# Three of four normalised row pairs of each attention batch, turned by VectorE blocks and device memory instead of by TensorE

## The chip, the cores and the metric

The kernel runs on one core of a Trainium2 chip. The metric is the device time of one execution in microseconds (us). The core has a matrix engine (TensorE, PE), a vector engine (VectorE, DVE), a scalar engine (ScalarE, ACT), GpSimd (POOL), and SyncE (SP), which here issues every transfer. Each engine works through its own program in order, and they wait for each other by semaphores.

## The reference

One hybrid layer over 2 batches of 1024 tokens with 512 columns, kept in float32:

```python
x = x + attn_a(_layernorm(x))     # gated linear attention, in chunks of 128 tokens
x = x + ffn(_layernorm(x))        # first feed-forward
x = x + attn_b(_layernorm(x))     # softmax attention, 1 head of 512 columns
x = x + ffn(_layernorm(x))        # second feed-forward, the same weights
```

where `attn_b` is

```python
scores = jnp.einsum('bqe,bke->bqk', Q, K) * scale
attn = jax.nn.softmax(scores, axis=-1)
out = jnp.einsum('bqk,bke->bqe', attn, V)
return jnp.einsum('bse,ed->bsd', out, W_o)
```

and `ffn` is `qlinear(silu(gate) * up)` with a hidden width of 1408.

## The kernel before

The program runs through stages: A (linear attention, both batches), F1 (feed-forward, batch 0 and 1), B (softmax attention, batch 0 and 1), F2 (feed-forward, batch 0 and 1). A float32 operand is split into a high and a low float16 part, and each product is three matmuls (high by high, high by low, low by high). The scores and the first feed-forward products use a recursive scheme of seven block products ("pieces" 1 to 7) in which sums and differences of the column blocks of an operand stand in for it.

Every stage takes its rows normalised and turned (features on partitions). One batch is 8 row tiles of 128 tokens, taken as 4 pairs (`i` = 0 to 3, two rows per pair). Six sets of pairs exist: F0, F1, B0, B1, F2, F3. For a pair, DVE takes row statistics (`x_stats`, three instructions), POOL the inverse deviation (`x_rstd`), DVE normalises both rows into the tile `xn` (`x_normalise`), the pair is turned, ACT takes its high parts (`x_row_highs`, `x_12_high`, `x_34_high`), DVE and POOL form differences and low parts (`x_second`, `x_34_low` on DVE; `x_sums`, `x_ab_low`, `x_12_low` on POOL).

There are two ways to turn. In the sets of `MOVED` (F1, B0, F3, prepared beside a feed-forward stage), DVE transposes 32x32 blocks in place, and SP sends the blocks to device memory and fetches them back in turned order, four DMAs out and four back (a "set" of four each way). In F0, B1 and F2, TensorE turns the pair: `turn_x` is four 128x128 transposes into one PSUM bank for each of the two rows (`turn_both(i)` is both), and ACT first copies the first row out of PSUM (`x_copy`).

B1 is prepared while batch 0 is in stage B, and F2 while batch 1 is. In stage B every engine's order is written out by hand, the same for both batches. For each of 8 query tiles there is a tile of probabilities: TensorE forms the scores (`first_row(p)` is pieces 1, 2, 6, 5, 3 for the tiles 2p and 2p + 1, then `score(7, p)` and `score(4, p)`), ACT and DVE add the pieces in `probs[i % 2]` (`part_sum`, `part_add`), DVE takes the row maximum, ACT the exponential (`softmax(i)`), DVE the block transpose (`p_blocks(i)`), SP sends it out and back, ACT and DVE split it (`pT_high`, `pT_low`), and TensorE multiplies it with the values (`attend(i)`). Piece 1, 6, 7 and 4 share PSUM bank 4, which is free again when the `part_sum` of the piece before has run. SP's queue holds the transfers of the probability tiles in strict order: out, wait, back.

## Time and profile before

| | before |
|---|---|
| median of 3 runs | 935.93 us (935.61 to 936.5) |
| the profiled execution's own time | 935.47 us |
| its span, first to last instruction | 933.7 us |
| PE busy | 919.0 us (98%) |
| DVE busy | 632.7 us (68%) |
| ACT busy | 444.5 us (48%) |
| POOL busy | 432.9 us (46%) |
| stage B, batch 0 and batch 1 | about 479 to 599 us and 604 to 719 us of the span |

The span leaves out some 1.8 us around the first and the last instruction. "Busy" is the time in which an engine had an instruction in work; a wait inside a stage shows as a gap in the timeline, with the instruction that ended it.

### The profile page before, as it was taken

What the parts mean: (1) busy time and instruction counts of PE and PEld (TensorE: products, weight loads), DVE (VectorE), ACT (ScalarE), POOL (GpSimd) and SP (SyncE); (2) the same over time, 40 slices, a digit from 0 to 9 for tenths busy, and PEclk for the clock granted to TensorE, in tenths of its full rate; (3) what the DMA queues carried; (4) which work ended last, traced back from release to release, by engine and by line L of the source; (5) the groups of instructions that cost most, each with busy time, mean ns of one, the idle gap of its engine ahead of it and who ended that gap; (6) DMA issues with size and microseconds to landing.
All of it is one profiled execution on the core that took longest, in us unless ns stands there. A gap on an engine that the chain in (4) does not pass through costs nothing.

```text
span 933.7 us, 13067 instructions
## 1 busy us (share of the span) xinstructions
PE 919.0 (98%) x4550; PEld 512.7 (55%) x4550; DVE 632.7 (68%) x1171; ACT 444.5 (48%) x884; POOL 432.9 (46%) x448
## 2 busy tenths in 40 slices
PE   7999999999999999999999999999999999999998
PEld 4888988888743444444444444444444444444444
DVE  7555656948777687777755878547786777765643
ACT  4433334356577723764333345324454685346620
POOL 5433524377446654665640144420535566546530
PEclk9999999999999999999999999999999999999999
DMA  9401300024031181003713637216371001910001
GB/s 319 179 12 35 136 24 24 1 90 138 25 111 46 24 131 28 1 11 63 109 46 56 104 53 147 48 26 97 59 113 24 1 1 32 194 45 1 1 34 57
DMA packets 239952, 61.75 MB, mean 66 GB/s; under 512 B 226768, under 2 KB 227088, under 8 KB 239504
## 3 DMA queue, kind: packets, MB, share of 16 engines
q1 hardware_dynamic: 239888, 60.92, 29.1%
q8 instruction: 37, 0.61, 0.3%
q14 instruction: 27, 0.22, 0.1%
HBM read 41.47 MB, written 19.43 MB: 65 GB/s over the span
## 4 chain that ended last, share of the span: by engine, by line
PE 85%; DVE 7%; POOL 2%; ACT 2%; issue 2%; DMA 1%; SPq 0%; DVEq 0%; ACTq 0%; POOLq 0%
PE psum L2327 49%; PE psum L2574 14%; PE psum L2576 14%; PE psum L2724 6%; DVE ln_bn L1620 1%; PE psum L2376 1%; DVE even_lo L2211 1%; PE psum L2461 1%; PE psum L2365 1%; DVE probs L2207 1%; DVE s_f L2155 0%; ACT probs L1493 0%; DVE wv_lo L1711 0%; DMA xres<-x 0%; DVE smax L2200 0%
## 5 line engine op out<-in xcount | busy, mean ns | idle before, releaser
L1038 POOL TENSOR_TENSOR hid<-hid,hid_hi 128x512 f32<-128x512 f32 x88 | 102.8, 1169 | 103.9 <-DVE hid_hi L1976 103.9
L2574 PE MATMUL psum<-xf,w_gu 128*128 128x512 f16 x352 | 133.8, 380 | 0.5 <-DVE yt L2058 0.5
L2574 PE MATMUL psum<-xf,w_s 128*128 128x512 f16 x264 | 100.1, 379 | 1.5 <-DVE up L1949 1.3
L2576 PE MATMUL psum<-xf,w_gu 128*128 128x512 f16 x264 | 100.1, 379 | 0.0
L2327 PE MATMUL psum<-wd_low,hid_lo 128*128 128x512 bf16 (+1 forms) x330 | 73.8, 373 | 0.0
L1361 ACT ACTIVATE hid_lo<-hid 128x512 f16<-128x512 f32 x88 | 54.9, 624 | 33.2 <-POOL hid L1038 33.2
L1034 POOL TENSOR_TENSOR hid<-up,gate 128x512 f32<-128x512 f32 x44 | 56.0, 1273 | 25.3 <-ACT gate L1356 25.3
L2576 PE MATMUL psum<-xq,w_s 128*128 128x512 f16 x176 | 66.7, 379 | 0.0
L2574 PEld LDWEIGHTS psum<-xf,w_gu 128*128 128x128 f16 x352 | 34.3, 98 | 55.0 <-ACT acc L1346 15.5
L1356 ACT ACTIVATE gate<-gate,sg_xs 128x512 f32<-128x512 f32 x44 | 31.7, 721 | 58.5 <-DVE gate L1959 58.5
L2327 PEld LDWEIGHTS psum<-wd_low,hid_lo 128*128 128x128 f16 x330 | 32.3, 98 | 36.8
L1941 DVE TENSOR_TENSOR gate<-psum,acc 128x512 f32<-128x512 f32 x44 | 30.4, 692 | 31.2 <-ACT acc L1334 23.5
L1976 DVE TENSOR_SCALAR hid_hi<-hid 128x512 f16<-128x512 f32 x88 | 39.1, 444 | 16.0 <-POOL hid L1034 14.5
L900 POOL TENSOR_TENSOR xrstd<-xvar,minus_half 128x1 f32<-128x1 f32 x48 | 25.2, 550 | 52.5 <-DVE xvar L1624 52.4
L2327 PE MATMUL psum<-wd_b,hid_hi 128*128 128x512 bf16 (+1 forms) x198 | 48.1, 373 | 0.0
L2574 PEld LDWEIGHTS psum<-xf,w_s 128*128 128x128 f16 x264 | 25.9, 98 | 35.7 <-issue 4.7
L1959 DVE TENSOR_TENSOR gate<-psum,acc 128x512 f32<-128x512 f32 x44 | 30.4, 691 | 20.4 <-PE psum L2576 20.1
L2576 PEld LDWEIGHTS psum<-xf,w_gu 128*128 128x128 f16 x264 | 25.8, 98 | 30.8
L1968 DVE SCALAR_TENSOR_TENSOR hid<-psum,su_c,gate 128x512 f32<-128x512 f32 x44 | 33.0, 750 | 12.5 <-PE psum L2576 12.5
L2327 PE MATMUL psum<-wd_a,hid_hi 128*128 128x512 bf16 (+1 forms) x165 | 39.9, 373 | 0.0
L2058 DVE TENSOR_TENSOR yt<-psum,sd_rows 128x512 f32<-128x512 f32 x31 | 21.1, 688 | 27.6 <-PE psum L2327 27.2
L1949 DVE SCALAR_TENSOR_TENSOR up<-psum,su_c,acc 128x512 f32<-128x512 f32 x44 | 33.0, 749 | 9.1 <-POOL hid L1034 7.6
(354 smaller groups left out, 2417.5 us busy)
## 6 DMA issues: line engine op xcount, KB each, us to landing
prob_blocks<-probs SPq DMA_DIRECT2D x60, 128.0 KB, 2.7
back<-prob_blocks SPq DMA_DIRECT2D x40, 128.0 KB, 2.8
turned<-blocks SPq DMA_DIRECT2D x36, 128.0 KB, 3.0
cla_wide<-cla_dram SPq DMA_DIRECT2D x16, 256.0 KB, 3.2
out<-xres SPq DMA_DIRECT2D x15, 256.0 KB, 2.0
xres<-x SPq DMA_DIRECT2D x3, 1024.0 KB, 12.9
blocks<-xn SPq DMA_DIRECT2D x24, 128.0 KB, 3.0
codes_gu<-gateT SPq DMA_DIRECT2D x1, 2816.0 KB, 11.7
```

Source lines behind the costliest of these rows:

```text
L1034: nc.gpsimd.tensor_tensor(hid2[:, :], up2[:, :], gate2[:, :], ALU.mult).then_inc(hid2_done, 1)
L1038: nc.gpsimd.tensor_tensor(hid[:, :], hid[:, :], hid_part(hid_hi, j, half), ALU.subtract).then_inc(rest_done, 1)
L1356: nc.scalar.activation(gate2[:, :], gate2[:, :], ACT.Silu, scale=sg_xs[:, j:j + 1]).then_inc(silu2_done, 1)
L1361: nc.scalar.activation(hid_part(hid_lo, j, half), hid[:, :], ACT.Copy, scale=LO).then_inc(lo_done, 1)
L1941: nc.vector.tensor_tensor(cols(gate1, j % 2), bank(2), acc1[:, :], ALU.add).then_inc(drained[2], 1)
L1949: nc.vector.scalar_tensor_tensor(out=up2[:, :], in0=bank(3 + j % 2), scalar=su_c[:, j:j + 1], in1=acc3[:, :], op0=ALU.mult, op1=ALU.add).t ...
L1968: nc.vector.scalar_tensor_tensor(out=hid1[:, :], in0=bank(j % 2), scalar=su_c[:, j:j + 1], in1=cols(gate1, j % 2), op0=ALU.mult, op1=ALU.m ...
L1976: nc.vector.tensor_scalar(hid_part(hid_hi, j, half), hid[:, :], ROUND, -ROUND, ALU.add, ALU.add).then_inc(hi_done, 1)
L2327: return nc.tensor.matmul(out, lhsT, rhs, start=start, stop=stop)
L2574: nc.tensor.matmul(bank(use[0]), w, x_operand(piece, k, False), start=start and k == 0, stop=False, skip_group_check=not start)
L2576: last = nc.tensor.matmul(bank(use[0]), w, x_operand(piece, k, True), start=False, stop=k == 1, skip_group_check=not start)
L2724: last = nc.tensor.matmul(bank(use[0]), l, r, start=start and k == 0 and j == 0, stop=k == 1 and j == 2, skip_group_check=not start)
```

## The change

For the pairs 0, 1 and 2 of B1 and F2 (`SENT = 3`) the transposes of TensorE go. DVE transposes the blocks of `xn` in place (`pair_turned`), SP sends them to a new buffer in device memory (`pair_to_dram`) and fetches them into the tile `x_first` of the set, which is made two rows wide (`pair_to_slot`); both rows are then read from there and no longer from PSUM. There is one such tile per set, so pair 1 is fetched only when all readers of pair 0 are done. Pair 3 is turned by TensorE as before. The normalised tile `xn` is still the only one, so each pair's `x_normalise` waits until the pair before has gone out. The second half of the new tile of B1's set covers `sd_rows`, which is therefore loaded a second time (`down_scales`). The orders of SP, DVE, ACT, POOL and PE in stage B are rewritten around it.

```diff
+SENT = 3
+            def pair_to_slot(q, i):
+
+                n = 4 * q + i
+                sp.wait_ge(pair_out, sent_all(q, i))
+                if i > 0:
+                    sp.wait_ge(x_ab_lo, n)
+                    sp.wait_ge(x_t34_done, 2 * n)
+                    sp.wait_ge(pair_2_lo, sent_n(q, i))
...
             query_parts(0, 0)
-            x_rstd(B1, *range(4))
+            x_rstd(B1, *range(6))
             query_parts(0, 1)
-            x_rstd(B1, *range(4, 8))
+            x_rstd(B1, *range(6, 8))
             pairs_of(B1)
...
+            def pair_turned(q, i):
+                dve.wait_ge(ln_xn_done, ln_n("X", q, 2 * i + 1) + 1)
+                nc.vector.transpose(xn[:, :], xn[:, :]).then_inc(pair_blocks_done, 1)
+
             def x_normalise(q, i):
+                if q in (B1, F2) and i > 0:
+                    dve.wait_ge(pair_out, sent_all(q, i - 1))
...
                 attend(1)
-                turn_both(0)
                 first_row(2)
                 attend(2, 0, 4)
                 score(7, 2)
                 attend(2, 4, 8)
                 score(4, 2)
-                turn_both(1)
                 first_row(3)
                 attend(3)
-                turn_both(2)
                 attend(4, 0, 4)
```

On PE the three `turn_both` go from each batch and nothing else moves. Three other places follow, all in batch 0; batch 1 has the same rows with its own tiles.

The queue of SP from the sending of probability tile 2 on, before (`probs_205` and `probs_206` are the two tiles `probs`, `back_207` and `back_208` those they come back to; x4 is one set of four DMAs):

```order
L854 DMA prob_blocks<-probs_205 32x32x32 x4
L865 DMA back_207<-prob_blocks 128x8x32 x4
L854 DMA prob_blocks<-probs_206 32x32x32 x4
L865 DMA back_208<-prob_blocks 128x8x32 x4
L854 DMA prob_blocks<-probs_205 32x32x32 x4
L865 DMA back_207<-prob_blocks 128x8x32 x4
```

and now (`x_first_141` is the two rows wide tile of set B1):

```order
L873 DMA prob_blocks<-probs_205 32x32x32 x4
L896 DMA pair_blocks<-xn 32x32x32 x4
L888 DMA back_207<-prob_blocks 128x8x32 x4
L873 DMA prob_blocks<-probs_206 32x32x32 x4
L896 DMA pair_blocks<-xn 32x32x32 x4
L912 DMA x_first_141<-pair_blocks 128x8x32 x4
L888 DMA back_208<-prob_blocks 128x8x32 x4
L896 DMA pair_blocks<-xn 32x32x32 x4
L912 DMA x_first_141<-pair_blocks 128x8x32 x4
L873 DMA prob_blocks<-probs_205 32x32x32 x4
L888 DMA back_207<-prob_blocks 128x8x32 x4
```

Between tile 2 and tile 4 the queue gets three sets out and two sets back for the pairs, and the fetch of pair 1 stands ahead of the sending of tile 4.

The order of ACT from the exponential of tile 4 to the score piece 1 of the tiles 6 and 7, before (L1488 is `part_sum`, L1493 `softmax`):

```order
L1493 ACTIVATE probs_205,rowsum<-probs_205,nmax,mids 128x1024
L1488 ACTIVATE probs_206<-psum 128x512 x2
L1488 ACTIVATE probs_205<-psum 128x512
L1493 ACTIVATE probs_206,rowsum<-probs_206,nmax,mids 128x1024
L1488 ACTIVATE probs_205<-psum 128x512
L1156 ACTIVATE x_first_141<-psum 128x512
```

and now (L1566 is `part_sum`, L1571 `softmax`, L1245 and L1247 are the high parts of pair 1):

```order
L1571 ACTIVATE probs_205,rowsum<-probs_205,nmax,mids 128x1024
L1566 ACTIVATE probs_206<-psum 128x512
L1245 ACTIVATE xb_hi_57<-x_first_141 128x4x128
L1247 ACTIVATE xb_hi_57<-x_first_141 128x4x128
L1566 ACTIVATE probs_206<-psum 128x512
L1566 ACTIVATE probs_205<-psum 128x512
L1258 ACTIVATE xs_hi_61<-x_mid_145 128x4x128
```

The two copies of pair 1 now stand between the two `part_sum` of `probs_206`, that of piece 7 and that of piece 4.

The order of DVE from the first `part_add` of the tiles 4 and 5 on, before (L1665 to L1670 are `x_second(0)`, L2188 and L2190 `part_add`):

```order
L2190 TENSOR_TENSOR probs_205<-psum,probs_205 128x512
L1665 TENSOR_TENSOR x_mid_145<-psum,x_first_141 128x256
L1668 TENSOR_TENSOR x_mid_145<-psum,x_mid_145 128x256
L1670 TENSOR_TENSOR xb_lo_59<-psum,xb_hi_57 128x4x128
L2188 TENSOR_TENSOR probs_205<-psum,probs_205 128x512
L2190 TENSOR_TENSOR probs_205<-psum,probs_205 128x512
L2200 TENSOR_REDUCE smax<-probs_205 128x1
L2202 TENSOR_SCALAR nmax<-smax,mids 128x1
L1630 TENSOR_SCALAR xn<-xres,xmv,xrstd 128x512 x2
```

and now (L1752 to L1757 are `x_second(0)`):

```order
L2277 TENSOR_TENSOR probs_205<-psum,probs_205 128x512
L1752 TENSOR_TENSOR x_mid_145<-x_first_141 128x256
L1755 TENSOR_TENSOR x_mid_145<-x_first_141,x_mid_145 128x256
L1757 TENSOR_TENSOR xb_lo_59<-x_first_141,xb_hi_57 128x4x128
L1698 BN_STATS ln_bn<-xres 128x6
L1700 BN_AGGR xmv<-ln_bn 128x2
L1702 TENSOR_SCALAR xvar<-xmv 128x1
L1698 BN_STATS ln_bn<-xres 128x6
L1700 BN_AGGR xmv<-ln_bn 128x2
L1702 TENSOR_SCALAR xvar<-xmv 128x1
L2275 TENSOR_TENSOR probs_205<-psum,probs_205 128x512
L2277 TENSOR_TENSOR probs_205<-psum,probs_205 128x512
```

The statistics of the last two rows, which stood with those of the rows 4 and 5 ahead of the query parts, now come behind `x_second(0)`. On POOL the inverse deviations of these rows stand ahead of `x_sums(0)` in both kernels.

## Rows read from the trace of the kernel before

**Rows 1.** The page, part 1: busy time, share of the span, instructions.

```profile
PE 919.0 (98%) x4550; PEld 512.7 (55%) x4550; DVE 632.7 (68%) x1171; ACT 444.5 (48%) x884; POOL 432.9 (46%) x448
```

**Rows 2.** Waits of PE: us in total, times, longest.

```profile
PE psum L2327 <- DVE even_lo L2211: 2.3, 3, 0.8
```

**Rows 3.** Groups by line and shape, PE: busy us, mean ns, idle before.

```profile
L2376 PE MATMUL psum<-ident,xn 128*128 128x128 f32 x96 | 13.5, 274 | 0.5 <-DVE a_lo L2159 0.5
```

**Rows 4.** Timeline of PE: start us, us, count, idle before.

```profile
4.05 4.45 PE L2327 MATMUL psum<-mask_b,ident_b 128*128 128x512 bf16 x10 [4.05 <-POOL mask_b L941]
...
515.31 0.38 PE L2724 MATMUL psum<-xb_hi,s_lo 128*128 128x512 f16 x1
516.51 0.38 PE L2327 MATMUL psum<-v_hi,even_hi 128*128 128x512 f16 x1 [0.82 <-DVE even_lo L2211]
...
539.81 0.60 PE L2376 MATMUL psum<-ident,xn 128*128 128x128 f32 x4
...
541.11 0.38 PE L2724 MATMUL psum<-xb_hi,a_hi 128*128 128x512 f16 x1
...
555.36 1.04 PE L2376 MATMUL psum<-ident,xn 128*128 128x128 f32 x8
556.30 0.38 PE L2724 MATMUL psum<-xb_hi,a_hi 128*128 128x512 f16 x1
```

**Rows 5.** Timeline of DVE, batch 0 of stage B.

```profile
530.08 0.65 DVE L1620 BATCH_NORM_STATS2 ln_bn<-xres 128x6 f32<-128x512 f32 x1
...
534.10 0.42 DVE L2152 SCALAR_TENSOR_TENSOR s_f<-psum,a_f 128x256 f32<-128x256 f32 x1
...
537.57 1.87 DVE L2155 TENSOR_TENSOR s_f<-s_f,a_f 128x256 f32<-128x256 f32 x1
...
539.82 0.68 DVE L2159 SCALAR_TENSOR_TENSOR a_lo<-psum,a_hi 128x512 f16<-128x512 f32 x1
...
550.70 1.00 DVE L1630 TENSOR_SCALAR xn<-xres,xmv,xrstd 128x512 f32<-128x512 f32 x2
552.18 1.25 DVE L2207 STREAM_TRANSPOSE probs<-probs 128x1024 f32<-128x1024 f32 x1 [0.49 <-ACT probs L1493]
...
555.05 0.21 DVE L2221 TENSOR_SCALAR mids<-rowsum,mids 128x1 f32<-128x1 f32 x1
...
556.16 0.68 DVE L2190 TENSOR_TENSOR probs<-psum,probs 128x512 f32<-128x512 f32 x1
```

**Rows 6.** Timeline of POOL, batch 0 of stage B.

```profile
536.62 2.55 POOL L1102 TENSOR_TENSOR s_lo<-s_f,s_hi 128x1024 f16<-128x1024 f32 x1 [2.72 <-ACT s_hi L1472]
...
541.07 2.13 POOL L1102 TENSOR_TENSOR s_lo<-s_f,s_hi 128x1024 f16<-128x1024 f32 x1 [1.10 <-ACT s_hi L1472]
...
544.67 0.54 POOL L900 TENSOR_TENSOR xrstd<-xvar,minus_half 128x1 f32<-128x1 f32 x1
545.46 0.73 POOL L910 TENSOR_TENSOR x_last<-x_mid,x_first 128x256 f32<-128x256 f32 x1 [0.25 <-DVE x_mid L1668]
...
547.95 1.15 POOL L923 TENSOR_TENSOR xs_lo<-x_mid,xs_hi 128x512 f16<-128x512 f32 x1
```

**Rows 7.** `x_mid` with both inputs in SBUF: ns min/median/max, first and last start.

```profile
L1665 DVE TENSOR_TENSOR x_mid<-turned x9: 382/424/426, 340.1 to 813.1; 128x256 f32<-128x256 f32 x9
L1665 DVE TENSOR_TENSOR x_mid<-xn x3: 1160/1195/1195, 357.9 to 819.0; 128x256 f32<-128x256 f32 x3
```

**Rows 8.** Timeline of SP's queue and of ACT: sets of four DMAs, their readers.

```profile
444.24 4.12 SPq L820 DMA_DIRECT2D turned<-blocks  x4
...
450.66 0.63 ACT L1167 ACTIVATE xb_hi<-turned 128x512 f16<-128x512 f32 x1 [2.33 <-DMA turned<-blocks]
...
555.55 0.60 ACT L1488 ACTIVATE probs<-psum 128x512 f32<-128x512 f32 x1 [2.93 <-PE psum L2724]
...
557.86 2.43 SPq L865 DMA_DIRECT2D back<-prob_blocks  x4
...
562.89 1.06 ACT L1503 ACTIVATE even_hi<-back 128x1024 f16<-128x1024 f32 x1 [0.43 <-DMA back<-prob_blocks]
```

146 lines of the change are left out of this document (106 added, 40 removed).

## The prediction

> **What bounds the kernel now.** I read the busy shares first: PE works for 919.0 of the 933.7 us of the span [rows 1], so time can only be won by taking work from PE or ending one of its few waits, and every new wait of PE is paid in full. Then the waits of PE: in stage B, where the change lies, there are three for `pT_low`, 2.3 us together [rows 2]. Then the timeline of PE through batch 0 of stage B, which shows what a `turn_both` takes there, from the first transpose to the next matmul: 1.30 us for pair 0 (539.81 to 541.11, a wait included) and 0.94 us for pair 1 (555.36 to 556.30) [rows 4]. Last the other engines around these places, for how much later than needed each would come if PE were earlier. Batch 1 has the same order and repeats the pattern; I work out batch 0 in the clock of this trace.
>
> **What the change removes from PE.** Three of eight pairs go per batch: 48 of the 96 transposes at L2376, of 13.5 us busy [rows 3]. On the path I take 1.30 us for pair 0 and 0.94 us for pair 1 and, as the nearest row, for pair 2: 3.18 us per batch, 6.36 us in all.
>
> **The waits for `pT_low`.** Two of the three stand ahead of `attend(0)`, one per batch. The last matmul before it starts at 515.31 and has a slot of 0.22 us, so PE could go on at 515.52; it does at 516.51: 0.98 us [rows 4]. `pT_low(0)` was behind `x_stats` of two rows, and now stands ahead of them. Four rows of statistics take 4.02 us (530.08 to 534.10) [rows 5], so it comes 2.0 us sooner, and both waits go: 1.96 us. The third, 2.3 less 2 x 0.82 = 0.65 us, is ahead of `attend(6)` of batch 0, behind the fetch of tile 6; it goes too if the chain of the tiles is not later, with 0.7 us. So 6.36 + 1.96 + 0.7 = 9.0 us would be gained if nothing new waited.
>
> **What it adds.** DVE gets six block transposes; one of 128x1024 takes 1.25 us, 1.17 to the next start [rows 5]: 7 us, on an engine that is idle for a third of the span. ACT loses six copies. SP gets 12 sets of four DMAs (48) and one load of 256 KB. None of these is paid as such; the question is what waits for them. I follow the two places where PE could stop.
>
> **First place: `score(6, 2)`, after `attend(1)`.** Its left operand is the last `s_lo` of POOL, which before ended at 543.20 (541.07 + 2.13) [rows 6]; PE came at 543.70, since the pieces 1 and 2, twelve matmuls of 0.216 us or 2.59 us, began at 541.11 [rows 4]. The chain to it starts on DVE with the first query part, at 534.10 before [rows 5], behind four rows of statistics. Now two of these rows are gone from there (2.0 us), `x_normalise(1)` with 1.0 us and two transposes with 2.3 us are added, and some 1.9 us of DVE's waiting for exponentials, and the move of `x_normalise(0)` into one of them, are filled; counted row by row DVE comes to the query parts at 532.7, 1.4 us sooner, and PE's own queries are 0.98 us sooner, which is soon enough. So the last query part ends at 539.1 instead of 540.5 (539.82 + 0.68) [rows 5], and the last `s_lo` could start at 539.7 instead of 541.07; DVE's `x_normalise(2)` is then in its second half, so I let it start at 540.0 and end at 542.2. PE, 0.98 us sooner and without the turn, ends `attend(1)` at 538.83, does the pieces 1 and 2 (2.59 us) and arrives at 541.4: it waits 0.8 us.
>
> That POOL waits for DVE here is read from the rows: `s_lo` took 2.55 us beside DVE's two-input work and 2.13 us alone, and DVE's L2155 took 1.87 us and ended at 539.44, just behind the end of `s_lo` at 539.17 [rows 5, 6]. The Trainium skill says the same (GPSIMD Engine Reference, Specifications): the two share their way into SBUF when VectorE reads two SBUF inputs. This speaks against the change: `x_second` read PSUM and SBUF before and now reads two tiles in SBUF. Its nearest rows are the sets turned through device memory: 0.38 to 0.43 us, and 1.16 to 1.20 us with POOL in its way [rows 7]. POOL is idle at the new `x_second(0)`, so I take the first; 0.75 us is the upper bound.
>
> **Second place: `score(1, 3)`, behind pair 1.** This is what decides. Bank 4 must be emptied of piece 4 by `part_sum`, and on ACT the high parts of pair 1 now stand ahead of that `part_sum`; they wait for the fetch of pair 1, which waits on SP for POOL's readers of pair 0, since there is one tile. Step by step:
> - DVE ends the query parts at 539.1, then `x_normalise(2)` 1.0, its transpose 1.17, `out_add(1)` 1.11 (555.05 to 556.16) [rows 5], `part_add` 0.61: 543.0.
> - `x_second(0)` 1.4: 544.4. Statistics of the last two rows 2.0: 546.4.
> - POOL may not begin `x_sums(0)` at 543.9, since the inverse deviation of row 7, 0.54 us [rows 6], stands ahead of it: 547.0. `x_sums(0)` and `x_ab_low(0)` take 2.5 us (545.46 to 547.95) [rows 6]: 549.5.
> - SP issues the set for pair 1. From the first issue to the reader's start a set took 5.03 us where the reader waited for it alone (557.86 to 562.89) and 6.42 us in a stretch of sets back to back (444.24 to 450.66) [rows 8]. Few transfers are near here; I take 5.2: 554.7.
> - ACT: two high parts 1.1, `part_sum` 0.6, 0.15 to PE (555.55 to 556.30 with its own 0.60) [rows 4, 8]: 556.5.
>
> PE arrives much sooner. From 542.2 it has the work that lay between 543.70 and the turn of pair 1 at 555.36 [rows 4], 11.66 us: 553.9. So it waits 2.6 us, and goes on at 556.5, where it went on at 556.30 before. All that was gained up to here in the batch (0.98 + 1.30 + 0.94) is given back, and 0.2 us more.
>
> **After it.** Counted on with the same durations, `pT_low(4)` ends 1.0 us before `attend(4)` wants it, `pT_low(5)` 2 us, `pT_low(6)` 1.5 us. Tile 4's transfers stand behind those of pair 1 on SP: issued from 552.0, out of the tile by 556.5, and ACT writes into that tile next at 557.8, when piece 1 of the next tiles is done. So the third turn (0.94) and in batch 0 the wait before `attend(6)` (0.7) are kept. The feed-forward that follows gets its last pair from TensorE as before, as much sooner as PE is.
>
> **The sum.** Batch 0: +0.2 - 0.94 - 0.7 = -1.44. Batch 1: +0.2 - 0.94 = -0.74. Together -2.2 us against the profiled execution's own 935.47, so 933.3; that execution lies 0.46 us under the median of 935.93, so the median after should be 933.7. I give 933.8. A change of 0.2% (1.9 us, under 934.06 or over 937.8) is about what a measurement of this kernel can tell from no change; the forecast is hardly past it.
>
> **The rivals.**
> 1. *Nearly all is gained.* If the fetch of pair 1 landed by 552, ACT would not hold PE, and only the wait of 0.8 us per batch were left: 9.0 - 1.6 = 7.4 us, 928.5. For it: pair 0 could be read by POOL 3 us sooner, and the transfers are idle. Against it: the inverse deviation of row 7 stands ahead on POOL, and I find no way for it to come before 546.9. Something between, with the chain a microsecond or two shorter than I count it because DVE is ahead of my count, is as likely: each microsecond gives 2. Together 0.21, at about 930.5.
> 2. *The sets are slow.* With 6.42 instead of 5.2 us for the fetch, 1.2 us later per batch: +0.2, so 936.1, no change. For it: between 530 and 541 five sets now stand nearly back to back, where two were, and `x_second(0)` needs one of them. Against it: the fetch of pair 1 itself comes 6 us later. 0.15.
> 3. *Slower: the fetch of pair 1 comes so late that its wait passes the gain.* Place and mechanism as above; it turns to a loss when ACT has the pair more than 1.1 us later than 554.7 in each batch, and is slower by 0.2% from 2.0 us later. That is so when the last `s_lo` gets the way into SBUF first and holds `x_normalise(2)`, the head of this chain, for its 2.13 us [rows 6]: +2.1 per batch, +2.0 in all, 937.9. For it: the two would start within 0.6 us of each other. Against it: DVE is first by my count. 0.15.
> 4. *The clock of PE falls in the new wait.* Right after its wait of 4.05 us at the start PE ran ten 128x512 matmuls in 4.45 us [rows 4], 0.43 us each as at 1.2 GHz; at the later pace of 0.22 us they take 2.3 us. So 2.1 us per fall, twice 4.3: 938.0. Against it: the wait is 2.6 us, and the 0.98 us waits did nothing to the pace. 0.05. The Trainium skill warns of it (TensorE: Matmul & The Clock Gate, Why this matters for your kernels): long idle gaps between bursts of matmuls bring the lower clock back. No wait of PE in stage B of this trace is long enough to show it.
>
> **How the numbers follow.** The forecast has 0.44, with a range of its own of 932.5 to 935.0, since the fetch has 5.03 us as one bound (-0.3) and `x_second` 0.75 us per batch as the other (+1.5, cut at half, POOL being idle). About 0.27 of it lie under 934.06. Faster by over 0.2%: 0.27 + 0.21 = 0.48. Within 0.2%: 0.17 + 0.15 = 0.32. Slower: 0.20. Up to 938.0 the slower cases are taken in, and down to 929.8 most of the first rival.
>
> **What would show it.** PE's waits in stage B: those on `even_lo` gone or under 0.3 us; two new ones of 2 to 3 us for `probs` of ACT ahead of `score(1, 3)`, and two of about 0.8 us for `s_lo` of POOL. The transposes at L2376's successor are 48, PE busy some 6.7 us less. ACT waits for the transfer from `pair_blocks` ahead of the second pair's high parts. DVE busy 7 us more. I am wrong if PE goes on at `score(1, 3)` a microsecond or more before or after 556.5 in the clock of this trace, or if `attend(4)`, `attend(5)` or `attend(6)` waits for its tile.

## The result and the profile after

The changed kernel takes 941.58 us (median of 4 runs, 940.77 to 942.51); the kernel before took 935.98 us in the same session (4 runs). The ratio is 1.0052, with a 95% interval of 1.0040 to 1.0065: slower by 0.5% (0.6% by the two medians). The forecast was 933.8 us, 0.2% faster. The profiled execution takes 941.07 us with a span of 939.3 us, 5.6 us more than before.

PE has less to do, as intended: the transposes fell by half, from 13.5 us to 6.9 [rows 3]. Its busy time fell by only 3.1 us, from 919.0 [rows 1] to 915.9, mostly because some matmuls ran slower, as shown below. From the page, and from the groups by line of PE:

```profile
PE 915.9 (98%) x4486; PEld 506.8 (54%) x4502; DVE 638.6 (68%) x1177; ACT 441.9 (47%) x878; POOL 431.8 (46%) x448
```

```profile
L2468 PE MATMUL psum<-ident,xn 128*128 128x128 f32 x48 | 6.9, 273 | 0.0
```

The waits of PE (us in total, times, longest) show what came for it. The three for `even_lo` [rows 2] are gone; these four groups stand in stage B:

```profile
PE psum L2816 <- ACT probs L1566: 6.7, 3, 3.8
...
PE psum L2816 <- POOL s_lo L1174: 1.3, 2, 0.7
PE psum L2855 <- ACT probs L1571: 1.2, 1, 1.2
...
PE psum L2816 <- POOL a_lo L1172: 0.6, 2, 0.5
```

The timeline of PE through stage B (start, duration, idle time before), to be laid beside [rows 4]:

```profile
515.26 0.38 PE L2419 MATMUL psum<-v_hi,even_hi 128*128 128x512 f16 x1
...
538.90 0.39 PE L2816 MATMUL psum<-xb_hi,a_hi 128*128 128x512 f16 x1 [0.17 <-POOL a_lo L1172]
...
542.34 0.39 PE L2816 MATMUL psum<-xs_hi,s_hi 128*128 128x512 f16 x1 [0.67 <-POOL s_lo L1174]
...
553.87 0.38 PE L2816 MATMUL psum<-xs_hi,a_hi 128*128 128x512 f16 x1 [0.99 <-ACT probs L1566]
...
554.94 0.38 PE L2816 MATMUL psum<-xs_hi,a_lo 128*128 128x512 f16 x1
559.14 0.59 PE L2816 MATMUL psum<-xb_hi,a_hi 128*128 128x512 f16 x1 [3.82 <-ACT probs L1566]
...
565.00 0.38 PE L2816 MATMUL psum<-xs_hi,s_lo 128*128 128x512 f16 x1
...
685.91 0.38 PE L2816 MATMUL psum<-xb_hi,a_hi 128*128 128x512 f16 x1 [1.91 <-ACT probs L1566]
...
713.01 1.09 PE L2855 MATMUL psum<-ident,probs 128*128 128x128 f32 x8 [1.19 <-ACT probs L1571]
```

`attend(0)` starts without a wait at 515.26. `score(1, 3)` starts at 559.14 in batch 0, after 3.82 us, and at 685.91 in batch 1, after 1.91 us. The 0.99 us ahead of 553.87, in front of `score(4, 2)`, was not forecast either, but it costs nothing by itself: without it PE would have waited that much longer for pair 1. From 559.14 to 565.00 there are 14 matmuls at 0.42 us each, where 0.22 is the pace. The windows of batch 0 say why (columns: stretch and its length in us, busy us of PE, PEld, DVE, ACT and POOL, then the granted clock as a share of full speed, the DMA share, GB/s):

```profile
552.00:556.00 4.00, 2.33 (x11) 0.71 (x8) 2.95 (x3) 1.72 (x3) 1.61 (x2) 1.00 0.69 109
556.00:560.00 4.00, 0.86 (x3) 0.34 (x4) 1.89 (x4) 1.63 (x3) 0.96 (x1) 0.76 1.00 154
560.00:564.00 4.00, 4.00 (x11) 1.42 (x10) 1.60 (x3) 2.11 (x3) 2.86 (x4) 0.50 0.64 103
564.00:568.00 4.00, 4.00 (x17) 1.66 (x16) 2.85 (x5) 2.16 (x5) 0.24 (x1) 0.88 0.44 71
```

The granted clock is 0.50 of full speed, the 1.2 GHz level, in the stretch behind the 3.82 us wait. The twelve matmuls of pieces 1 and 2 take 5.07 us and the next twelve, pieces 6 and 5, 2.95, instead of 2.59 each: 2.84 us in all.

**Where the 5.6 us are.** The execution after is 0.27 us ahead when stage B's first scores of the tiles 2 and 3 begin (508.70 against 508.97). Batch 0 then loses 4.55 us up to batch 1's first matmul (608.47 against 604.19), batch 1 loses 0.95 up to the feed-forward (724.30 against 719.07), and the feed-forward 0.37, which was not followed further: 4.55 + 0.95 + 0.37 - 0.27 = 5.6.

**What made pair 1 late.** DVE, POOL, SP and ACT in batch 0, and DVE and POOL at the same place in batch 1:

```profile
539.75 2.81 DVE L1714 TENSOR_SCALAR xn<-xres,xmv,xrstd 128x512 f32<-128x512 f32 x2 [0.39 <-DMA pair_blocks<-xn]
539.94 2.34 POOL L1174 TENSOR_TENSOR s_lo<-s_f,s_hi 128x1024 f16<-128x1024 f32 x1 [1.10 <-ACT s_hi L1550]
...
546.23 0.68 DVE L1757 TENSOR_TENSOR xb_lo<-x_first,xb_hi 128x512 f16<-128x512 f32 x1
...
549.01 0.54 POOL L972 TENSOR_TENSOR xrstd<-xvar,minus_half 128x1 f32<-128x1 f32 x1 [0.47 <-DVE xvar L1702]
...
550.89 1.16 POOL L989 TENSOR_TENSOR xb_lo<-x_first,xb_hi 128x512 f16<-128x512 f32 x1
552.11 2.62 SPq L912 DMA_DIRECT2D x_first<-pair_blocks  x4
...
557.36 0.63 ACT L1245 ACTIVATE xb_hi<-x_first 128x512 f16<-128x512 f32 x1 [3.64 <-DMA x_first<-pair_blocks]
...
669.13 0.99 DVE L1714 TENSOR_SCALAR xn<-xres,xmv,xrstd 128x512 f32<-128x512 f32 x2
669.78 2.33 POOL L1174 TENSOR_TENSOR s_lo<-s_f,s_hi 128x1024 f16<-128x1024 f32 x1 [1.10 <-ACT s_hi L1550]
```

The two halves of `x_normalise(2)` took 2.81 us in batch 0, since POOL's `s_lo` began 0.19 us after the first and held the second, and 0.99 in batch 1, where DVE had 0.65 us of lead: there the second half, which starts 0.46 us behind the first, was already running. In batch 0 DVE had first waited 0.39 us for pair 1 to have gone out of `xn`; in batch 1 it did not wait. Everything behind follows at the predicted distances: the low part of pair 0 ends at 552.05, SP issues at 552.11, ACT has pair 1 at 557.36 (5.25 us; forecast 5.2), and PE goes on 1.78 us later (forecast 1.8).

### The profile page after: what moved, and what is told of

The parts are those of the page before. It is cut to its first block, busy times and chain, and to the rows that moved or that the text cites. A ratio compares the mean times of both kernels' runs of the same rounds, so it can differ in the third digit from the quotient of the medians.

```text
span 939.3 us, 13002 instructions
## 1 busy us (share of the span) xinstructions
PE 915.9 (98%) x4486; PEld 506.8 (54%) x4502; DVE 638.6 (68%) x1177; ACT 441.9 (47%) x878; POOL 431.8 (46%) x448
## 4 chain that ended last, share of the span: by engine, by line
PE 69%; SPq 9%; DVE 8%; DMA 5%; POOL 3%; issue 3%; ACT 2%; DVEq 0%; POOLq 0%; ACTq 0%
PE psum L2419 38%; PE psum L2666 14%; PE psum L2668 13%; PE psum L2816 3%; SPq L820 2%; SPq L873 2%; SPq L839 2%; SPq L888 1%; DMA prob_blocks<-probs 1%; DMA bq_col<-bq 1%; DVE probs L2294 1%; SPq L912 1%; DMA probs<-prob_blocks 1%; PE psum L2553 1%; DMA turned<-blocks 1%
## 5 line engine op out<-in xcount | busy, mean ns | idle before, releaser
L2419 PE MATMUL psum<-wd_b,hid_hi 128*128 128x512 bf16 (+1 forms) x190 | 45.8, 373 | 0.2
L2419 PE MATMUL psum<-wvo,xb_hi 128*128 128x512 f16 x128 | 38.1, 379 | 0.0
```

Source lines behind the costliest of these rows:

```text
L2419: return nc.tensor.matmul(out, lhsT, rhs, start=start, stop=stop)
```

## The experiments

Each was timed against the kernel before on the same chip (medians of 935.45 to 935.77 us; the changed kernel itself against 935.98). Differences between two rows carry both errors, so the ratios are the safer comparison. "Before" and "changed" name the two kernels.

| run | kernel and change | us | ratio to before, 95% |
|---|---|---|---|
| e1_act_order | changed, ACT: high parts of pair 1 behind two `part_sum` | 945.28 | 1.0110, 1.0095 to 1.0124 |
| e2_pool_order | changed, POOL: two inverse deviations behind the low parts of pair 0 | 936.58 | 1.0004, 0.9996 to 1.0013 |
| e3_filled_wait | changed, 14 idle matmuls in the wait of batch 0 | 939.72 | 1.0045, 1.0029 to 1.0060 |
| e4_before_low_first | before, DVE: `part_add(2, 1)` and `pT_low(0)` ahead of two statistics | 933.76 | 0.9982, 0.9973 to 0.9990 |
| e5_chain_short | changed, the chain to pair 1 shortened on POOL, DVE and SP | 936.44 | 1.0006, 0.9997 to 1.0015 |
| e5b_slot2_early | e5_chain_short, pair 2 fetched ahead of tile 5 | 939.47 | 1.0042, 1.0030 to 1.0054 |
| e6_one_pair | only pair 0 sent | 933.49 | 0.9979, 0.9970 to 0.9988 |
| e7_long_runs | changed, pairs moved in runs of 1024 bytes and not turned | 932.06 | 0.9964, 0.9952 to 0.9976 |
| e8_both_filled | changed, 14 idle matmuls in the wait of both batches | 939.16 | 1.0039, 1.0026 to 1.0052 |
| e9_turn_behind_piece | e4_before_low_first, second turn behind piece 1 | 935.40 | 1.0000, 0.9992 to 1.0009 |
| e10_normalise_later | changed, `x_normalise(2)` behind `part_add(2, 2)` | 941.91 | 1.0065, 1.0052 to 1.0078 |
| e11_one_pair_max6 | e6_one_pair, tile 6 earlier on DVE and ACT | 934.24 | 0.9988, 0.9979 to 0.9997 |
| e12_short_long | e5_chain_short, moved as in e7_long_runs and not turned | 932.77 | 0.9972, 0.9960 to 0.9983 |
| e13_tile4_first | e5_chain_short, tile 4 ahead of pair 2 | 937.79 | 1.0024, 1.0014 to 1.0034 |
| e14_load_only | e4_before_low_first, with sets that nothing reads | 945.81 | 1.0111, 1.0097 to 1.0125 |
| e15_load_long | e14_load_only in runs of 1024 bytes | 943.94 | 1.0096, 1.0080 to 1.0111 |
| e16_load_free | e14_load_only without SP's wait ahead of the sixth set | 936.24 | 1.0003, 0.9994 to 1.0012 |
| e17_best | e11_one_pair_max6, transpose of tile 6 earlier | 932.89 | 0.9969, 0.9958 to 0.9981 |

### What holds ACT

```diff
                 part_sum(7, 2)
-                x_row_highs(q, 1)
                 part_sum(4, 2)
                 part_sum(1, 3)
+                x_row_highs(q, 1)
```

> On ACT the two high parts of pair 1 stand behind the two part_sum of pieces 4 and 1 instead of ahead of them; nothing else moves. Theory A (ACT's queue held PE, and nothing else does): the waits of 3.8 and 1.9 us ahead of score(1, 3) go, the slow matmuls after the first with them (2.8 us), and most of it stays: 933 to 935. Theory B (the late pair 1 holds DVE as well, where x_second(1) stands ahead of part_add(5, 2), and the tiles 5 and 6 come late through SP's queue): PE then waits for DVE's part_add ahead of piece 5 until about 560.2, about 1.9 us, and for pT_low(5) ahead of attend(5), so that only some 1.5 us are won in batch 0 and about 0.2 in batch 1: 939.9. I hold B.

945.28 us: slower than the changed kernel by 3.7, so theory A is false. B forecast a small gain and is wrong too, in the direction: its wait for `part_add` is there (1.24 us of the 1.9), but PE also waits 2.21 us for a `part_sum` and 1.31 us for `pT_low(4)` in batch 0, with the granted clock at 1.00. Timelines of ACT and PE:

```profile
555.55 0.60 ACT L1566 ACTIVATE probs<-psum 128x512 f32<-128x512 f32 x1 [1.64 <-PE psum L2816]
560.51 0.60 ACT L1566 ACTIVATE probs<-psum 128x512 f32<-128x512 f32 x1 [4.37 <-DMA prob_blocks<-probs]
561.00 0.62 ACT L1245 ACTIVATE xb_hi<-x_first 128x512 f16<-128x512 f32 x1
...
561.25 0.38 PE L2816 MATMUL psum<-xs_hi,s_hi 128*128 128x512 f16 x1 [2.21 <-ACT probs L1566]
```

The first `part_sum` of the next tiles writes into the tile from which tile 4 is still being sent. It waited 4.37 us for that, and pair 1, whose fetch SP had issued at 552.30, 2.65 us ahead of tile 4's sending, now stood behind it. So there are two late things at this place, pair 1 and the sending of tile 4, and the order on ACT only chooses between them.

### The chain to pair 1

```diff
             query_parts(0, 1)
-            x_rstd(B1, *range(6, 8))
             pairs_of(B1)
...
                     x_12_low(q, i)
+                    if q in (B1, F2) and i == 0:
+                        x_rstd(q, 6, 7)
```

> On POOL the inverse deviations of the rows 6 and 7 stand behind the low parts of pair 0 instead of ahead of its sums; nothing else moves. If the chain that makes pair 1 late is x_second(0), two statistics, inverse deviation, sums: the sums of pair 0 start at about 546.3 instead of 549.5, SP issues pair 1 at 549, ACT has it at 554.2 instead of 557.4, PE goes on at score(1, 3) at 556 instead of 559.1 with a wait under 1 us and full pace in batch 0, without a wait in batch 1, and the tiles 4 to 6 are sent sooner too: 933 to 935. If pair 1 is late because the transfers are slow, the landing moves by less than 1 us: 940 to 941.5.

936.58 us: 5.0 us won by the place of four small instructions of POOL. `x_normalise(2)` took 2.81 us here too. SP issues pair 1 1.9 us sooner than in the changed kernel and ACT has it 2.3 us sooner, though this execution was 0.9 us behind that one when these scores began:

```profile
550.19 2.60 SPq L912 DMA_DIRECT2D x_first<-pair_blocks  x4
...
555.06 0.63 ACT L1245 ACTIVATE xb_hi<-x_first 128x512 f16<-128x512 f32 x1 [0.52 <-DMA x_first<-pair_blocks]
```

PE's longest wait in stage B is 1.13 us, ahead of `turn_last`, and the clock 1.00 throughout. The expectation was met but for batch 1, where 0.78 us of wait stayed, and for the time, 1.6 us over its upper end; what remained was looked for in the later runs. So the long wait goes without touching `x_normalise(2)`: there was enough slack to win elsewhere in the chain.

```diff
-                x_normalise(q, 2)
-                pair_turned(q, 2)
                 out_add(1)
 
                 part_add(2, 2)
+                x_normalise(q, 2)
+                pair_turned(q, 2)
```

> The changed kernel with x_normalise(2) and its transpose behind out_add(1) and part_add(2, 2) on DVE, so that they begin when POOL's s_lo ends. Theory: in the changed kernel x_normalise(2) and s_lo start within some 0.3 us of each other; where POOL is first, x_normalise(2) takes 2.81 us, where DVE has 0.65 us of lead, 0.99. Here it is never over 1.2 us. Against a batch where they met, x_second(0) starts 1.0 us sooner, against one where they did not, 1.3 us later; so both batches now have a wait of 3 us or more ahead of score(1, 3) and slow matmuls behind it: 941 to 943, with less spread. If the meeting is not what makes the pair late, no change in the spread: 941.6.

941.91 us, with a granted clock of 0.994 to 0.998 over the span in every run, as expected. In the profiled execution PE waits 3.60 us in batch 0 and 3.24 in batch 1 ahead of `score(1, 3)`, and the clock falls behind both. POOL and DVE of batch 0:

```profile
541.64 2.12 POOL L1174 TENSOR_TENSOR s_lo<-s_f,s_hi 128x1024 f16<-128x1024 f32 x1 [1.10 <-ACT s_hi L1550]
544.00 0.99 DVE L1714 TENSOR_SCALAR xn<-xres,xmv,xrstd 128x512 f32<-128x512 f32 x2
```

In the profiled executions with the changed kernel's order here, `x_normalise(2)` took 2.81 us five times and 2.94 once where DVE led by 0.07 to 0.33 us, and 0.99 six times where it led by 0.65 us or more; in this run, behind `s_lo`, 0.99 twice. DVE was first in all twelve, so the expectation had the order wrong. What parts the two groups is DVE's wait ahead of it: in each of the six that were held DVE had waited 0.23 to 0.49 us for pair 1 to have gone out, in the other six it had not waited. This run takes the meeting away but moves the instruction behind two others, so it shows what the meeting does to `x_normalise(2)` and not what its end alone would win. The Trainium skill names such a meeting (GPSIMD Engine Reference, Specifications): besides instructions with two SBUF inputs, VectorE's contend with GpSimd for SBUF when they run in a mode that uses both ports. By that rule `x_normalise`, which reads one tensor from SBUF, is held if it runs in such a mode; the trace shows that it is held, and not the mode.

The next runs shorten the chain at all its links (DVE, then SP; POOL's order is that of e2_pool_order):

```diff
+                out_add(1)
+
+                part_add(2, 2)
+                x_second(q, 0)
                 x_normalise(q, 2)
                 pair_turned(q, 2)
-                out_add(1)
-
-                part_add(2, 2)
-                x_second(q, 0)
+                part_add(3, 2)
+                row_max(4)
                 x_stats(q, 6)
                 x_stats(q, 7)
-                part_add(3, 2)
-                row_max(4)
...
+                        pair_to_slot(s, 1)
                         pair_to_dram(s, 2)
-                        pair_to_slot(s, 1)
```

> All three pairs sent, with the chain to pair 1 shortened: POOL's inverse deviations of the rows 6 and 7 behind the low parts of pair 0; on DVE x_second(0) ahead of x_normalise(2) and its transpose, and the statistics of the rows 6 and 7 behind row_max(4); on SP the fetch of pair 1 ahead of the sending of pair 2. If the late pair 1 and the late softmax(4) are all that the change lost: x_normalise(2) no longer meets POOL's s_lo, pair 1 is fetched from 546.5 and is there at 552, no wait ahead of score(4, 2) and score(1, 3), full pace, and only the 0.7 us for s_lo stays; what is left is the wait for tile 6 ahead of attend(6), 1 to 2 us in batch 0: 933.1. If the sets themselves crowd the queue, the tiles 5 and 6 come late as before: 935 to 936.

Against this kernel, e5b_slot2_early changes SP's order once more:

```diff
-                        probs_to_dram(b, 5)
                         pair_to_slot(s, 2)
+                        probs_to_dram(b, 5)
```

> As e5_chain_short, and on SP the fetch of pair 2 ahead of the sending of tile 5 instead of behind it. If the fetch of pair 2 is what delays the sending of tile 6 (it stands between tile 5 out and tile 5 back), the waits ahead of attend(6) in batch 0 and of turn_last in batch 1 shrink by 1 us or more each: 931 to 932. If the fetch now waits for POOL's readers of pair 1 and holds tile 5 behind it: slower than e5_chain_short by up to 2 us.

e5_chain_short takes 936.44 us: no better than POOL's order alone, and 0.4 us over the second expectation, the crowded queue. The wait for pair 1 is gone, and PE has two others at this place in batch 0:

```profile
555.78 0.38 PE L2816 MATMUL psum<-xb_hi,a_hi 128*128 128x512 f16 x1 [0.78 <-ACT probs L1566]
...
560.09 0.38 PE L2816 MATMUL psum<-xs_hi,s_hi 128*128 128x512 f16 x1 [1.57 <-ACT probs L1566]
```

The second is tile 4 again: it is sent from 554.48, 1.3 us ahead of `score(1, 3)`, where before it was sent 2.85 us ahead (553.45). On DVE the pairs' work stands ahead of the tile's transpose, and on SP the sending of pair 2 ahead of the tile's; e13_tile4_first, below, moves both. With pair 2's fetch ahead of tile 5 (e5b_slot2_early) it is 939.47: the fetch was issued at 561.35, and tile 5 went out at 565.09 instead of 562.99. It is slower, as the other branch said, by 3.0 us where that allowed 2.

### What the turn had hidden

The wait ahead of `score(1, 3)` is never under 0.78 us in a batch that has neither a turn nor other matmuls there, and 0.78 wherever pair 1 is in time. The next kernel puts a turn behind that piece.

```diff
                 score(4, 2)
-                turn_both(1)
-                first_row(3)
+                score(1, 3)
+                turn_both(1)
+                for piece in (2, 6, 5, 3):
+                    score(piece, 3)
```

> e4_before_low_first (933.8) with turn_both(1) behind score(1, 3) instead of ahead of it. In every kernel without a turn there, PE waits 0.78 us for part_sum to empty bank 4 between score(4, 2) and score(1, 3), and 0.60 us between pieces elsewhere; the turn's 0.94 us hid it. If so, this kernel waits about 0.78 us ahead of score(1, 3) in each batch and does the turn besides, which now hides the hand-over from piece 1 to piece 6, already hidden by piece 2: 1.6 us more, 935.3. If the 0.78 us comes from something that the pairs' transfers delay, no wait appears: 933.8.

935.40 us, 1.6 us over e4_before_low_first, as expected. PE, in a kernel that sends no pair at all:

```profile
556.07 0.38 PE L2723 MATMUL psum<-xb_hi,a_hi 128*128 128x512 f16 x1 [0.78 <-ACT probs L1488]
```

So of the 0.94 us of `turn_both(1)` only 0.16 was to be had. While PE turned, ACT emptied bank 4.

### The lower clock

```diff
+                def warm(count):
+                    u.free((0, 7 if b == 0 else 6))
+                    for _ in range(count):
+                        mm(bank(0), xb_hi[b][:, 0:P], xb_hi[b][:, 0:D], True, True)
...
                 score(4, 2)
+                warm(14)
                 first_row(3)
```

> 14 matmuls of 128x512 (3.0 us) whose result nobody reads are put on PE in batch 0 between score(4, 2) and first_row(3), into the long wait, so that PE is not idle for more than a microsecond; nothing else moves. If the slow pace after the wait is the lower clock that follows an idle stretch, the twelve matmuls of pieces 1 and 2 take 2.6 us each piece pair instead of 5.1 and 3.0, and PE reaches attend(3) 2.8 us sooner. If the pace were the end of the chain: 938.7. If tile 6 comes when it comes whatever PE does (its low part ends 0.06 us before attend(6)): at most 0.9 us are won: 940.7 to 941.5. I expect the second.

> The changed kernel with 14 matmuls of 128x512 (3.0 us), whose result nobody reads, ahead of first_row(3) in both batches. If PE's lower clock comes from the long wait there, the granted clock is 1.0 in every run and no matmul behind it is slow; the long wait stays as late as before for its releaser, and the time is that of the changed kernel less the 2.8 us of slow matmuls, with 0.5 to 1 us of it lost again to the wait for tile 6: about 939.5. If the slow pace had another cause, the clock stays at 0.996 to 0.998 and the time at 941 or more.

The code is that of e8_both_filled. In e3_filled_wait (batch 0 alone; another left operand) the runs lie between 936.0 and 942.4 us, median 939.72, which bears out neither expectation: in the profiled execution the wait to be filled was not in that batch. Its profile shows the opposite of the changed kernel's: no meeting of DVE and POOL in batch 0, one in batch 1, and there the long wait and slow matmuls.

```profile
664.37 2.94 DVE L1714 TENSOR_SCALAR xn<-xres,xmv,xrstd 128x512 f32<-128x512 f32 x2 [0.49 <-DMA pair_blocks<-xn]
664.44 2.12 POOL L1174 TENSOR_TENSOR s_lo<-s_f,s_hi 128x1024 f16<-128x1024 f32 x1 [1.10 <-ACT s_hi L1550]
...
683.24 0.38 PE L2816 MATMUL psum<-xb_hi,a_hi 128*128 128x512 f16 x1 [3.45 <-ACT probs L1566]
```

With both waits filled (e8_both_filled) the granted clock is 1.0 in five of six runs and 0.999 in one, and the time 939.16, near the 939.5 expected: 2.4 us less than the changed kernel by the medians, with more than a microsecond of doubt, as its runs lie between 938.1 and 941.8. That is the clock's share of the loss, and it was won with PE doing more.

### The transfers

```diff
-                dst = pair_slot(q)[:, :].rearrange("p (m a j) -> p m a j", a=QUADS, j=SQ)
+                rows = pair_blocks[sent_n(q, i)].rearrange("a m (x y) j -> (a m x) (y j)", y=SQ)
                 for a in range(QUADS):
-                    sp.dma_start(dst[:, :, a, :],
-                                 pair_blocks[sent_n(q, i), a].rearrange("m p j -> p m j")).then_inc(pair_back, 16)
+                    sp.dma_start(pair_slot(q)[:, a * 256:(a + 1) * 256], rows[:, a * 256:(a + 1) * 256]).then_inc(pair_back, 16)
```

> The changed kernel with the pairs' sets moved as plain copies: the same bytes in the same 24 + 24 transfers, but in runs of 1024 bytes instead of 128, so that the pairs are not turned (their scores are wrong, and nothing else changes). If the cost of the sets is in their number of small pieces, a pair's set takes some 3 us instead of 5.2 and the tiles' sets beside it are quicker too: x_normalise(2) no longer waits for pair 1 to go out and starts before POOL's s_lo in both batches, pair 1 is there some 4 us sooner in batch 0, and the wait ahead of score(1, 3) falls under 1 us: 934 to 935.5. If what counts is the order and the readers of the one tile, not the transfers, only 1 to 2 us are won: 939.5 to 940.5.

The sending of a pair is changed in the same way. This kernel leaves out the turning of the sent pairs, so its results are wrong: it prices the transfers and is no kernel to keep.

932.06 us, 9.5 less than the changed kernel (0.9% by the two ratios) and 2 under my lowest number. Every order is that of the changed kernel. DVE, SP and ACT, batch 0:

```profile
539.23 0.99 DVE L1712 TENSOR_SCALAR xn<-xres,xmv,xrstd 128x512 f32<-128x512 f32 x2
...
549.77 1.75 SPq L911 DMA_DIRECT2D x_first<-pair_blocks  x4
552.21 2.27 SPq L873 DMA_DIRECT2D prob_blocks<-probs  x4
...
553.75 0.63 ACT L1243 ACTIVATE xb_hi<-x_first 128x512 f16<-128x512 f32 x1 [2.36 <-DMA x_first<-pair_blocks]
...
556.82 3.23 SPq L888 DMA_DIRECT2D back<-prob_blocks  x4
```

Pair 1 is there 3.98 us after SP's first issue instead of 5.25; SP spends 1.75 us on a set instead of 2.62; tile 4 is out 4.61 us after its issue instead of 5.62 (554.77 to 560.39); and pair 1 had gone out before DVE wanted `xn`, so `x_normalise(2)` was ahead of POOL by 0.65 us or more in both batches. The wait ahead of `score(1, 3)` is 1.42 us in batch 0, not under 1, and 0.78 in batch 1. The Trainium skill expects this of small pieces (DMA: Bandwidth & Descriptors, Why small descriptors are slow (HBM only)): a cost per packet and per descriptor that long ones spread. By that rule 128-byte runs are the poor case, and the trace agrees. SP's shorter issue of a set is in the gain too, and no run separates the two.

> e5_chain_short (936.4) with the pairs' sets as plain copies in runs of 1024 bytes, as in e7_long_runs (the pairs are not turned, their scores are wrong). If the rest of the loss is the load of small pieces on the tiles' own sets, the waits for tile 4 out (1.6 and 0.4 us), for tile 6 (0.9) and of turn_last (1.6) shrink by 1 us each: 932 or less. If it is DVE's added work ahead of tile 4, 935 to 936.

The same edit on e5_chain_short, again with pairs that are not turned: 932.77 us, 3.7 less than with small pieces and between the two expectations. The wait of 1.57 us fell to 0.58, the one of `turn_last` from 1.6 to 0.5, the one ahead of `attend(6)` from 0.9 to 0.4. Most of what e5_chain_short had left to lose is due to the small pieces; the two 0.78 us remain. It is no faster than e7_long_runs.

The next kernel is e5_chain_short with tile 4 first, shown for DVE; on SP the sending of tile 4 moves ahead of that of pair 2, and the statistics of the rows 6 and 7 behind `row_max(5)`:

```diff
-                x_normalise(q, 2)
-                pair_turned(q, 2)
                 part_add(3, 2)
                 row_max(4)
-                x_stats(q, 6)
-                x_stats(q, 7)
+                x_normalise(q, 2)
                 p_blocks(4)
+                pair_turned(q, 2)
```

> e5_chain_short with tile 4 first: on DVE the transpose of tile 4 ahead of that of pair 2, the statistics of the rows 6 and 7 behind row_max(5), on SP the sending of tile 4 ahead of that of pair 2, on POOL the inverse deviations of these rows behind pair 1. Tile 4 is sent some 2 us sooner (552 instead of 554.5), so the wait ahead of piece 6 of the next tiles goes (1.6 and 0.4 us): 934.5 to 935 if DVE's work was the cause; 936 if the transfers take it back at the tiles 5 and 6.

937.79 us, slower than e5_chain_short and than either expectation. Tile 4 went out at 552.44 and the wait ahead of piece 6 did go; but PE then waited 0.65 and 0.38 us for `pT_low(4)`, 0.78 and 1.91 us for a `part_sum` that stands on ACT behind the fetches of pair 2 and tile 5, and for tile 6 0.77 us ahead of `attend(6)` in batch 0 and 1.13 ahead of `turn_last` in batch 1. The queue that was late at tile 4 was late at the tiles 5 and 6.

```diff
+            def load_only(b, k):
+                for a in range(QUADS):
+                    sp.dma_start(pair_blocks[6 * b + k, a].rearrange("m p j -> p m j"),
+                                 prob_blocks[b * BT, a].rearrange("m p j -> p m j")).then_inc(load_out, 16)
...
+                if i == 5:
+                    sp.wait_ge(x_ab_lo, 4 * s + 2)
+                    load_only(b, 5)
```

> e4_before_low_first (933.8), all pairs turned by TensorE, with six sets of four transfers per batch put into SP's queue where the changed kernel has its pairs' sets, of the same bytes in the same runs of 128 bytes, from device memory to device memory; nobody waits for them and nothing reads them. If the load alone delays the tiles: 936 to 938, with waits for probs of ACT ahead of the pieces of tile 6 and longer ones ahead of attend(6). If the transfers only cost where something waits for a pair: under 934.5.

> e14_load_only with the same bytes in runs of 1024 bytes. If the number of small pieces is what loads, 933.8 to 934.5 whatever e14_load_only gives; if it is SP's time to issue 24 more transfers per batch, the same as e14_load_only.

945.81 us is 8 over what was expected, and 943.94 is near it, which fits the second branch of e15_load_long but has another reason than SP's time to issue: they say little of load, and much of order. SP's queue in e14_load_only, and PE:

```profile
560.11 2.25 SPq L867 DMA_DIRECT2D prob_blocks<-probs  x4
567.64 2.71 SPq L853 DMA_DIRECT2D pair_blocks<-prob_blocks  x4
570.45 2.98 SPq L886 DMA_DIRECT2D back<-prob_blocks  x4
...
578.02 0.38 PE L2744 MATMUL psum<-xs_hi,a_hi 128*128 128x512 f16 x1 [3.72 <-ACT probs L1509]
```

SP stood at the sixth set from 562.4 to 567.6 for POOL's low part of pair 1, and tile 5's fetch stood behind it. In the changed kernel that wait guards the fetch of pair 2; here nothing needs it. Without it:

```diff
                 if i == 5:
-                    sp.wait_ge(x_ab_lo, 4 * s + 2)
                     load_only(b, 5)
```

> e14_load_only without the wait for POOL ahead of the sixth load set, which is issued as soon as SP comes to it, between tile 5 out and tile 5 back. Until that place e14_load_only ran as e4_before_low_first did. If the load of the sets costs only where something waits behind them, tile 5's fetch comes at about 564.5 as before and the time is 934 to 935; if it delays the tiles 5 and 6 by itself, waits ahead of attend(5), attend(6) or turn_last of 1 us or more appear: 936 or more.

936.24 us, 2.5 over e4_before_low_first (2.0 by the two ratios), which does the same work. SP and PE, batch 0:

```profile
552.03 2.62 SPq L867 DMA_DIRECT2D prob_blocks<-probs  x4
558.46 1.63 SPq L885 DMA_DIRECT2D back<-prob_blocks  x3
...
559.27 0.38 PE L2743 MATMUL psum<-xs_hi,s_hi 128*128 128x512 f16 x1 [1.64 <-ACT probs L1508]
```

Tile 4, sent right behind eight load transfers, was out after 6.43 us (before: 4.41, from 553.45 to the fetch at 557.86 [rows 8]), and PE waited 1.64 us for it. The expectation had the time right and the place wrong: it looked for waits at the tiles 5 and 6. So the load costs by itself, 2.0 to 2.5 us beside the 3.7 that e12_short_long gave back; its transfers go from device memory to device memory and not through SBUF.

### What can be kept

> The kernel before, with part_add(2, 1) and pT_low(0) ahead of the statistics of the rows 2 and 3 on DVE, as the change has them; all pairs turned by TensorE. The prediction's term for this was 0.98 us per batch: 934.0 if all of it stays; 935.0 if half of it turns into a wait for POOL's s_lo ahead of score(6, 2), which had 0.5 us to spare.

e4_before_low_first takes 933.76 us, 2.0 under the kernel before: the first branch. Two lines of DVE's order, without a transfer, are worth what was predicted of them.

> Only pair 0 of each batch is sent, the pairs 1 and 2 are turned by TensorE as in the kernel before, pT_low(0) ahead of the statistics, the statistics of the rows 6 and 7 behind row_max(4), and POOL's order as in e2_pool_order. It keeps the 0.98 us ahead of attend(0) and the 1.30 us of the first turn per batch, pays 0.7 us for s_lo, and has no fetch into an occupied tile: 1.5 us won per batch against the kernel before, and nothing lost later: 932.9. If the pair's two sets delay the probability tiles: 934 to 935, no better than e4_before_low_first.

933.49 us, with the one pair whose fetch finds its tile free. It is not to be told from e4_before_low_first, as the second branch said, though that put it at 934 or more: the turn's 1.30 us bought a wait of 0.4 to 0.5 us for `s_lo`, and 0.7 us more for tile 6 (1.19 against 0.50).

```diff
                 part_add(3, 3)
+                row_max(6)
                 x_second(q, 1)
                 pT_low(4)
-                row_max(6)
+                p_blocks(6)
                 out_add(3)
-                p_blocks(6)
```

The first half of this, with `softmax(6)` ahead of the high parts of pair 1 on ACT, is e11_one_pair_max6; both are e17_best.

> e6_one_pair (933.5) with row_max(6) ahead of x_second(1) and pT_low(4) on DVE, and softmax(6) ahead of the high parts x_12_high(1) and x_34_high(1) on ACT. Tile 6 is sent some 2 us sooner, and the wait of 1.2 us ahead of attend(6) in batch 0 goes, unless SP still has tile 5's fetch to issue; pT_low(4) may come up to 0.3 us late for attend(4): 932.3. If the transfers of tile 6 slip by as much as it is sooner, 933.5.

> e11_one_pair_max6 with the block transpose of tile 6 ahead of out_add(3) on DVE. In e11_one_pair_max6 the exponential of tile 6 was done at 565.5, but its transpose began at 567.9, behind out_add(3), which waits for attend(3); now it begins at 566.8. Tile 6 is sent 1 us sooner and the wait ahead of attend(6) in batch 0 falls from 1.4 to 0.4 us: 932.5 to 933. If its transfers slip again, 933.5 to 934.

934.24 us for the first: nothing won, the second branch or worse. The exponential of tile 6 began 2.5 us sooner than in e6_one_pair, and its transpose only 0.2:

```profile
564.13 1.24 ACT L1567 ACTIVATE probs<-probs,nmax,mids 128x1024 f32<-128x1024 f32 x1 [1.36 <-DVE nmax L2285]
...
567.85 1.24 DVE L2290 STREAM_TRANSPOSE probs<-probs 128x1024 f32<-128x1024 f32 x1
```

`out_add(3)` was ahead of it on DVE and waits for `attend(3)`. With the transpose ahead of it the wait before `attend(6)` is 0.15 us instead of 1.45, and the time 932.89 us, as expected, the lowest of the kernels that turn their pairs: 0.3% under the kernel before. Its interval overlaps that of e6_one_pair, so which of the two is faster is not shown.

## Why the prediction was wrong

The places, and most of the links between them, were right; one link was not, and what followed from it had been left out of the sum. By the prediction's own steps, in the clock of the trace of before (0.27 us added to times of after):

- **The wait ahead of `attend(0)`**: gone, 0.98 us per batch as forecast, and shown alone by e4_before_low_first (2.0 us for both).
- **First place, `score(6, 2)`**: forecast 542.2 after 0.8 us, measured 542.6 after 0.67 (and 0.17 for `a_lo`).
- **Second place, `score(1, 3)`: the step that failed.** Place, mechanism and the last three links were right. The link "`x_normalise(2)` 1.0" was not: DVE first waited 0.39 us for pair 1 to have gone out, a wait that the forecast put at nothing, and so met `s_lo`, 2.81 us. The twelve batches of the six kernels with this order show the two together (six with the wait, all held; six without, none held), and in e7_long_runs, where the pairs go out sooner, there is neither in either batch. With 0.5 us for query parts that ended later than counted, PE went on at 559.4 instead of 556.5: 2.9 us. No run takes the meeting alone away, so its 1.8 us of this is read from the trace and not from a time. In batch 1, where they did not meet, the place cost 0.32 us against 0.2 forecast. I had this as the third rival, at 0.15, "DVE is first by my count"; it was first, by 0.19 us, and being first was not enough. Where the meeting did not come about, the forecast of the place was good to 0.12 us.
- **PE's clock**: left out of the sum, and the fourth rival, at 0.05, at 2.1 us a fall. It fell in batch 0 and cost 2.84 us. Both rivals were one case and not two: the meeting makes the wait long (in this kernel's order, batch 0 here and batch 1 of e3_filled_wait), and behind the long wait the clock falls. I had added their chances as if each came alone. The meeting is not the only way to a long wait, though: e10_normalise_later has none, and waits of 3.60 and 3.24 us with a fall behind each.
- **After it**: `attend(4)` and `attend(5)` did not wait, and in batch 0 the third turn and the wait ahead of `attend(6)` gave 1.4 of the 1.64 us forecast. In batch 1 `turn_last` waited 1.19 us and 0.27 us was lost ahead of `score(4, 3)`: 1.57 us against the forecast. Tile 6 was sent as early in the batch as before, but was out only after 5.14 us instead of 4.39, right behind the fetches of pair 2 and tile 5 on SP. I had followed tile 6 to `attend(6)` and not to `softmax(7)`, which stands behind it on ACT.

Batch 0 came to +4.55 for -1.44, batch 1 to +0.95 for -0.74: 6.0 and 1.7 us over the forecast; the feed-forward's 0.37, less the 0.27 at the start, makes the 7.8 of the whole. The "9.0 us to be gained" was too high as well: e9_turn_behind_piece shows that the second turn was worth 0.16 us, not 0.94, since it hid the emptying of a bank. And "few transfers are near here" was right for pair 1 (5.25 us for 5.2) and wrong for the tiles: e16_load_free prices the sets at 2.0 to 2.5 us with nobody waiting for them, e7_long_runs the small pieces, with the meeting, the waits and the clock behind them, at 9.5. The lower end of the range, 932.5, had no term behind it: the fetch's bound of 0.3 us gives 933.5.

What stays open: why e12_short_long, with the shorter chain, is not faster than e7_long_runs; how much of the cost of small pieces is their transfer and how much SP's issue; and how the whole 5.6 us divides between the meeting and the slack that was missing behind it, since e2_pool_order wins 5.0 of them with the meeting still there in batch 0.

## What to carry to other kernels

Before work is taken from the bounding engine, look at what the other engines finish while it lasts: a turn of 0.94 us that hides a hand-over of 0.78 is worth 0.16. In a chain across several in-order queues, write down every wait that the new code has, those that look satisfied too; here one of 0.39 us, put at nothing, led to a link of 2.81 us instead of 1.0. Where instructions of DVE and POOL that were seen to hold each other start within a few tenths of a microsecond, count the link at its upper value and look at what the longer wait then triggers. Transfers with nobody waiting for them still cost (2.0 to 2.5 us here), if the bounding engine depends on others in the same queue; a wait at the head of that queue cost more than the bytes (945.81 us with it, 936.24 without).

## What the runs showed that I had not expected

- `x_normalise(2)`: 0.99 us alone or with 0.65 us of lead, 2.81 to 2.94 us when POOL's 2.1 to 2.3 us instruction begins 0.07 to 0.33 us after it.
- The lower clock does not follow the last wait's length alone. It fell after waits of 3.82, 3.60, 3.45 and 3.24 us, and in e5b_slot2_early at a wait of 1.99 us (granted 0.50 from 577 to 580), but not after 1.91 us in the changed kernel (1.00), nor after 3.12 us in batch 1 of e15_load_long (1.00), nor after 2.71 us in batch 1 of e5b_slot2_early (1.00). A fall cost 1.4 us in e10_normalise_later (3.99 us for 2.59) and 2.84 in the changed kernel. What else decides it is not shown.
- A set of four transfers of 128 KB each, tile 4's, took 4.4 us from issue to out alone, 5.6 behind one other set, 6.4 behind two. A pair's set of the same size took 5.25 us to its reader, and 4.0 in runs of 1024 bytes.
